# Expert products, gate logits and residual transposes in another order at the end of an attention layer

## What is computed

```python
def _L3_ffn_ref(x, gate_w, gate_b, w1, b1, w2, b2):
    scores = jnp.einsum('bsd,de->bse', x, gate_w) + gate_b
    probs = jax.nn.softmax(scores, axis=-1)
    topk_vals, topk_idx = jax.lax.top_k(probs, TOP_K)
    mask = jnp.sum(jax.nn.one_hot(topk_idx, NUM_EXPERTS, dtype=probs.dtype), axis=-2)
    masked = probs * mask
    masked = masked / (jnp.sum(masked, axis=-1, keepdims=True) + 1e-09)
    h = jax.nn.gelu(jnp.einsum('bsd,edh->ebsh', x, w1) + b1[:, None, None, :], approximate=False)
    y = jnp.einsum('ebsh,ehd->ebsd', h, w2) + b2[:, None, None, :]
    out = jnp.einsum('bse,ebsd->bsd', masked, y)
    return out
...
    t = t + _L3_attn_ref(_ln_t(t), L3_attn_qkv_w, L3_attn_qkv_b, L3_attn_out_w, L3_attn_out_b)
    t = t + _L3_ffn_ref(_ln_t(t), L3_ffn_gate_w, L3_ffn_gate_b, L3_ffn_w1, L3_ffn_b1, L3_ffn_w2, L3_ffn_b2)
```

## Time and profile before

| | us |
|---|---|
| median of three runs | 804.9 (804.72 to 805.72) |
| the profiled execution | 806.04 |
| its span, first to last instruction | 803.8 |
| TensorE busy in it | 743.9 (93%) |
| VectorE, ScalarE, POOL busy | 578.1, 571.6, 253.1 |
| mean granted clock of TensorE | 0.973 |

### The profile page before, as it was taken

The page is one execution under the profiler, slowest core; times in us unless marked ns, Lnnn a source line. Parts: engine busy times, 40 slices in busy tenths (PEclk is TensorE's granted clock), DMA queues, the critical chain, the costliest instruction groups (busy, mean ns, idle before and its releaser), DMA issues.

```text
span 803.8 us, 16948 instructions
## 1 busy us (share of the span) xinstructions
PE 743.9 (93%) x5265; PEld 583.6 (73%) x5265; DVE 578.1 (72%) x1415; ACT 571.6 (71%) x1425; POOL 253.1 (31%) x485
## 2 busy tenths in 40 slices
PE   1896999999999888999998986999999999999997
PEld 1874788788788776777776585677777786777775
DVE  6238677676777567788886798688888735877775
ACT  3323777977777557888886866688888748788785
POOL 1902155565554332121222000131212100544434
PEclk9999899999999999999999998899999959999999
DMA  6000000110110132333230002133333102223220
GB/s 218 1 1 0 1 7 17 20 16 18 20 17 16 26 90 74 90 90 104 80 103 17 0 1 80 51 99 88 102 94 89 29 1 82 50 59 76 63 50 20
DMA packets 60073, 41.36 MB, mean 51 GB/s; under 512 B 33904, under 2 KB 52464, under 8 KB 59888
## 3 DMA queue, kind: packets, MB, share of 16 engines
q1 hardware_dynamic: 60016, 40.63, 19.9%
HBM read 12.24 MB, written 3.21 MB: 19 GB/s over the span
## 4 chain that ended last, share of the span: by engine, by line
PE 77%; DVE 11%; ACT 4%; issue 3%; DMA 2%; SPq 2%; POOL 1%; POOLq 0%; DVEq 0%; ACTq 0%
PE ps L1236 11%; PE ps L990 10%; PE ps L1403 9%; PE ps L1418 8%; PE ps L1091 6%; PE ps L995 5%; PE ps L1075 3%; PE ps L1019 3%; PE ps L1033 3%; PE ps L998 2%; PE ps L1020 2%; SPq L309 2%; DMA qk<-hl 2%; PE ps L940 2%; DVE amax L1861 2%
## 5 line engine op out<-in xcount | busy, mean ns | idle before, releaser
L625 ACT ACTIVATE ee<-ps,nmax 128x128 f32<-128x128 f32 (+1 forms) x576 | 205.2, 445 | 11.5 <-DVE nmax L1592 6.4
L1236 PE MATMUL ps<-w,ee 128*128 128x128 f32 x960 | 134.8, 274 | 2.0 <-ACT big L612 1.9
L1236 PEld LDWEIGHTS ps<-w,ee 128*128 128x128 f32 x960 | 112.8, 143 | 13.6 <-ACT ee L625 2.8
L612 ACT ACTIVATE big<-ps 128x512 f32<-128x512 f32 (+1 forms) x192 | 96.6, 555 | 24.7 <-PE ps L1236 23.0
L1595 DVE TENSOR_REDUCE nmax<-ps 128x2 f32<-128x256 f32 x192 | 97.5, 550 | 13.5 <-PE ps L998 8.9
L1716 DVE TENSOR_TENSOR hhl<-ee,hhl 128x512 fp32r<-128x512 f32 x96 | 79.1, 829 | 33.1 <-ACT hhl L859 31.6
L990 PE MATMUL ps<-kh,big 128*128 128x256 f32 x384 | 94.7, 391 | 1.5 <-POOL big L385 1.2
L1592 DVE TENSOR_REDUCE nmax<-ps 128x4 f32<-128x1024 f32 x48 | 58.7, 1224 | 45.3 <-PE ps L990 45.1
L1403 PE MATMUL ps<-qk,w1hl 128*128 128x512 f32 x288 | 85.4, 405 | 0.0
L1418 PE MATMUL ps<-hhl,w2hl 128*96 128x512 f32 x288 | 82.4, 396 | 2.2 <-DVE big L1946 1.9
L529 POOL TENSOR_TENSOR xc<-big,xc 96x512 f32<-96x512 f32 x32 | 52.1, 1628 | 100.0 <-DVE big L1946 99.4
(11 more groups left out here) (260 smaller groups left out, 1333.2 us busy)
## 6 DMA issues: line engine op xcount, KB each, us to landing
qk<-hl SPq DMA_DIRECT2D x256, 96.0 KB, 3.1
big<-moe_gate SPq DMA_DIRECT2D x8, 768.0 KB, 6.9
w<-w_in SPq DMA_DIRECT2D x1, 1735.0 KB, 12.5
xc<-x_in SPq DMA_DIRECT2D x4, 384.0 KB, 5.6
l_mix<-on SPq DMA_DIRECT2D x32, 48.0 KB, 2.1
tok<-l_mix SPq DMA_DIRECT2D x16, 96.0 KB, 2.0
out<-xc SPq DMA_DIRECT2D x8, 192.0 KB, 2.1
w<-w_in SPq DMA_DIRECT2D x1, 998.0 KB, 8.8
```

The source lines that it names most:

```text
L612: nc.scalar.activation(et[:, h, 0:w], ps[:, 4 + hh, 0:w], ACT.Copy).then_inc(own(l, f"et{hh}"), 1)
L625: last = nc.scalar.activation(ee[:, ke, hh, qc, 0:w], src, ACT.Exp, bias=nmax[:, kp, hh, qc:qc + 1])
L1236: last = nc.tensor.transpose(ps[:, 4 + hh, b * P:(b + 1) * P], ee[:, u, hh, qc, tc * P:(tc + 1) * P], ident)
```

## The change

- TensorE's end of layer 3 follows a table, END_PE, in which three of the H stand between the other steps, and four of the R between the G; the O, C and P of image 15, B of images 14 and 15 and all G are in the table too. `hidden` is defined earlier for that. Four waits that stood in front of single steps stand in front of the table.
- The residual groups go in the order 0 to 7 with other banks; R4 stands before H3, R5 to R7 behind H3 to H5.
- ScalarE makes its split copies before its copy of the attention's result, and its residual copies of groups 0 and 1 after the copy by channel, groups 2 and 3 after the last `deviation`, 4 to 7 behind the first four Gelu pairs. VectorE makes its two `split_low` before it divides image 15.
- The first four gated sums stand in steps 12 to 15 instead of 14 to 17 (all later ones where they stood); the later `split_low` in the fifth step of a block instead of the third; T one pair later, VectorE's copy of it one low part later.
- SyncE waits for the first load of the gates before it issues the second.

```diff
-RES_ORDER = [0, 7, 1, 2, 3, 4, 5, 6]
-RES_BANK = [1, 1, 2, 3, 2, 1, 2, 3]
+RES_ORDER = [0, 1, 2, 3, 4, 5, 6, 7]
+RES_BANK = [1, 2, 3, 1, 2, 3, 2, 3]
+END_PE = ["H0", "O15", "G0", "C15", "H1", "B14", "R0", "P15", "G1", "R1", "H2", "G2", "R2", "G3", "R3", "G4", "B15", "G5", "G6", "G7"]
...
-            return max(NJ * k + 6, 14 + k)
+            return max(NJ * k + 6, 12 + k)
...
             load_gates(0)
+            sp.wait_ge(sg("moe_gates0"), 16)
             load_gates(1)
...
-                if l > 1:
-                    outputs_to_sbuf(l, B - 1)
-                    deviation(l, B - 2, 0)
-                if l == 3:
-                    residual_channels(0)
-                if l > 1:
-                    outputs_by_channel(l, B - 1)
                 if l == 3:
                     for par in range(2):
                         act.wait_ge(*upto(3, f"stacked{par}", STK * B // 2))
                     split_high(0)
                     split_high(1)
+                if l > 1:
+                    outputs_to_sbuf(l, B - 1)
+                    deviation(l, B - 2, 0)
+                    outputs_by_channel(l, B - 1)
+                if l == 3:
+                    residual_channels(0)
+                    residual_channels(1)
                     deviation(l, B - 1, 1)
-                    residual_channels(7)
+                    for g in range(2, 4):
+                        residual_channels(g)
...
-            residual_channels(1)
             for n in range(NS * NB):
...
-                if n < 5:
-                    residual_channels(n + 2)
+                if n < 4:
+                    residual_channels(n + 4)
...
-                    if l == 3:
-                        pe.wait_ge(*upto(l, "max", 3 * B))
-                        pe.wait_ge(*upto(l, "exp", 6 * B))
-                        gate_logits(0)
-                    outputs(l, B - 1)
+                    if l == 2:
+                        outputs(l, B - 1)
...
                 if l == 3:
-                    for g in range(2, 6):
-                        gate_logits(g)
-                    residual_rows(7)
-                    image_back(l, B - 1, 1)
-                    gate_logits(6)
-                    gate_logits(7)
+                    pe.wait_ge(*upto(l, "max", 3 * B))
+                    pe.wait_ge(*upto(l, "exp", 6 * B))
+                    pe.wait_ge(*upto(l, "v_sb", B))
+                    pe.wait_ge(sg("f3_wlo"), 1)
+                    for step in END_PE:
+                        what, n = step[0], int(step[1:])
+                        if what == "H":
+                            hidden(n)
+                        elif what == "G":
+                            gate_logits(n)
+                        elif what == "R":
+                            residual_rows(n)
...
             LAG = 3
-            pe.wait_ge(sg("f3_wlo"), 1)
             pe.wait_ge(sg("f3_w2lo"), 1)
-            for n in range(LAG):
-                hidden(n)
-                residual_rows(n + 1)
+            residual_rows(4)
             for n in range(LAG, NS * NB):
                 hidden(n)
+                if n < 6:
+                    residual_rows(n + 2)
                 expert_out(n - LAG)
-                if n < 6:
-                    residual_rows(n + 1)
-                if n == 6:
+                if n == 7:
                     pe.wait_ge(sg("f3_gate"), 1)
-                    pe.wait_ge(sg("xres"), res_done(3))
+                    pe.wait_ge(sg("xres"), 8)
                     nc.tensor.transpose(ps[:, 3, 0:P], gate[:, 0, :, :].rearrange("p t e -> p (t e)"), ident).then_inc(sg("moe_gate_ps"), 1)
-                if n == 9:
+                if n == 11:
                     pe.wait_ge(sg("moe_gate_t"), 1)
...
+                if l == 3:
+                    for t in range(2):
+                        split_low(t)
                 if l > 1:
                     normalise_outputs(l, B - 1)
...
-                    for t in range(2):
-                        split_low(t)
                     image_channels(l, B - 1)
...
-                if n == 4:
+                if n == 5:
                     dve.wait_ge(sg("moe_gate_ps"), 1)
                     V.tensor_copy(gate_t, ps[:, 3, 0:P]).then_inc(sg("moe_gate_t"), 1)
-                if n % NS == 2 and 1 <= n // NS < NB - 1:
+                if n % NS == 4 and 1 <= n // NS < NB - 1:
                     split_low(n // NS + 1)
```

More of the change, by code:

```diff
@@ L1172, in gate_logits, with hidden @@
                 last.then_inc(sg("f3_gl_ps"), 1)
+            def hidden(n):
+                t, s = n // NS, n % NS
+                if s == 0:
+                    pe.wait_ge(sg("moe_x"), t + 1)
+                if n >= 4:
+                    pe.wait_ge(sg("moe_hi"), n - 3)
+                for k, (w, x) in enumerate(((0, 0), (0, 1), (1, 0))):
+                    last = mm(ps[:, 4 + n % 4, :], w1hl[:, w, s * P:(s + 1) * P], xhl[:, t % 2, x, :], start=(k == 0), stop=(k == 2))
+                last.then_inc(sg("moe_h_ps"), 1)
             for l in (1, 2, 3):
@@ L1330, in _ @@
                     first_layer(0, 0)
-                if l == 3:
-                    gate_logits(1)
-                if l > 1:
+                if l == 2:
                     outputs_back(l, B - 1)
-                if l == 3:
-                    residual_rows(0)
-                if l > 1:
                     pe.wait_ge(*upto(l, "v_sb", B))
@@ L1341, in _ @@
                 if l == 3:
-                    for g in range(2, 6):
-                        gate_logits(g)
-                    residual_rows(7)
-                    image_back(l, B - 1, 1)
-                    gate_logits(6)
-                    gate_logits(7)
+                    pe.wait_ge(*upto(l, "max", 3 * B))
[10 more added lines that the diff above has]
+                            residual_rows(n)
+                        elif what == "O":
+                            outputs(l, n)
+                        elif what == "C":
+                            outputs_back(l, n)
+                        elif what == "B":
+                            image_back(l, n, n % 2)
+                        else:
+                            project_outputs(l, n)
                 if l > 1:
@@ L1395, in _ @@
                                 last.then_inc(sg("f2_y2_ps"), 1)
-            def hidden(n):
-                t, s = n // NS, n % NS
-                if s == 0:
-                    pe.wait_ge(sg("moe_x"), t + 1)
-                if n >= 4:
-                    pe.wait_ge(sg("moe_hi"), n - 3)
-                for k, (w, x) in enumerate(((0, 0), (0, 1), (1, 0))):
-                    last = mm(ps[:, 4 + n % 4, :], w1hl[:, w, s * P:(s + 1) * P], xhl[:, t % 2, x, :], start=(k == 0), stop=(k == 2))
-                last.then_inc(sg("moe_h_ps"), 1)
             def expert_out(n):
@@ L1414, in expert_out @@
                     pe.wait_ge(sg("f3_gl"), 1)
-                if j == 0 and t == 0 and 1 <= e <= 2:
-                    pe.wait_ge(sg("xres"), 6 + e)
+                if j == 0 and t == 0 and e > 0:
+                    pe.wait_ge(sg("xres"), max(res_done(g) for g in range(8) if RES_BANK[g] == e))
                 for k, (w, h) in enumerate(((0, 0), (1, 0), (0, 1))):
```

## The result

Five executions of the changed kernel have a median of 798.29 us (797.83 to 800.84), five of the kernel before beside them 804.72 (802.17 to 805.72). The ratio is 0.9938, with a 95% interval of 0.9922 to 0.9955: 5.0 us faster (3.6 to 6.3).

A forecast was written before the change was run, and what follows sets the result against it. TensorE, hardly ever without work from 640.50 us, was taken as the bound. -2.9 - 0.35 + 2.3 - 1.93 = -2.9 gave 803.1 from the profiled 806.04; the median 804.9 - 1.93 gave 802.97; forecast 803.0, range 801.0 to 805.2.

The forecast's parts named there:

- The wait before E(12), -1.93: TensorE's idle before E(12), waiting for the first gated sum, goes with the earlier gated sums: 1.93 us less, or 1.6.
- The order of the end: Layer 3's end on TensorE: early H delay the clock's fall to 651.43, last G ends at 655.27, E0 starts 2.9 earlier.
- gate chain: From the last G's end to E0, top-2 gate and low_part(0): 4.94 us plus 0.13, no longer covered by H and R.
- new wait: TensorE idle before E0, with only R4, H3 and R5 as cover: 2.2 us, or 3.6 at full clock.
- The clock after E0, +2.3: TensorE reaches E0 at half clock, and 3.2 to 5.7 us of products at half rate lose 1.6 to 2.9; 2.3 taken.
- first rival: The clock stays up through layer 3's end: 798.0 us on the median; falling but back by E0, near 800; chance 0.14.
- My two cases for its return: Full clock returns 3.2 us after gapless work from 478.0, or 5.7 us after dense products began at 656.37.
- the clock's terms: The sum's -2.9, -0.35 and +2.3 at layer 3's end, -0.95 together, left out when forecasting from the median.
- the sum: Whole kernel, from the profiled execution: -2.9 - 0.35 + 2.3 - 1.93 = -2.9 us, so 806.04 becomes 803.1.
- The second rival: The clock falls as early as before, H not holding it; last G ends at 660.7, total 807.5, slower; chance 0.10.
- the third one: Middle rival: the clock falls near 650, returns late, gate load takes 7.7; 805.4 us, no change; chance 0.26.
- The rule on transposes: Transposes don't count as clock activity like products, so only the H among the logits hold it; lowers the first rival's chance.

The follow-up runs named there:

- third profile of the same kernel: The changed kernel run a third time, nothing edited: median 798.89 us, ratio 0.9933 to the kernel before; its profiled execution took 801.92 us.
- steps alone: The kernel before with only the first four gated sums moved to steps 12 to 15: 801.63 us, ratio 0.9973.
- All but the steps: The changed kernel with the first four gated sums back in steps 14 to 17: 802.33 us, ratio 0.9974 to the kernel before.
- late H: The changed kernel with H0, H1 and H2 behind the last G again, run twice: 798.66 us (ratio 0.9934) and 799.24 us (0.9937).
- H and R both late: The changed kernel with H0 to H2 and R1 to R3 behind the last G, ScalarE's residual copies moved along: 799.18 us, ratio 0.9953.
- second profile of that kernel: The changed kernel run again, nothing edited: median 799.49 us, ratio 0.9936 to the kernel before; its profiled execution took 799.93 us.
- H3 three times: The changed kernel with H3 computed three times into the same bank before E0, R5 ahead of it: 797.58 us, ratio 0.9918.
- H2 late: The changed kernel with H2 alone moved behind the last G, into the wait before E0: 796.07 us, ratio 0.9903.

## Why the prediction was wrong

**The wait before E(12), -1.93: right.** Alone it brought 2.2, undone it cost 2.8. The gates came in time, a little sooner than I had worked out: the load landed near 676.4 and the first gated sum ran 8.71 after T (676.43 against 667.72), where I had the load landing 9.05 after it. VectorE waited for it, as I had said, though only 0.24 us.

**The order of the end: the mechanism right, the sizes small.** H0 came without a wait and takes 0.80 (O starts at 640.58), as priced. The clock fell 10.3 us after A, forecast 10.9. The last G ended 14.13 after A, forecast 14.77: G costs 0.81 between R (645.91 to 646.72), not 0.95. The gate chain took 5.02 from there to E0 (653.91 to 658.93), forecast 4.94 + 0.13. The new wait is 1.83, forecast 2.2; E0 came 19.15 after A, forecast 19.84. Against 22.73 before that is 3.6 earlier instead of 2.9.

**The clock after E0, +2.3: too much.** I had it low from the fall until some 4.6 us behind E0. In the changed kernel it was back before E0, at the end of R5, and then fell once more for 3.4 us, which costs 1.7. That is the first rival's last sentence (it falls and is back by E0: near 800), to which I had given part of 0.14; the profiled execution took 800.84. In the third profile of the same kernel it didn't come back, as forecast. My two cases for its return, 3.2 and 5.7 us, I had both called dense products. In the second, three H and two R stood in turn from 656.37 to 662.1, so it was no such case; and that it returns with only one H among transposes was in no row I had.

**The step that failed: the clock's terms, mis-sized in the sum and then put at nothing on the median.** On the profiled execution the sum gave -2.9; measured was -5.2. Of the 2.3 between them, 0.7 is A, which the change doesn't touch and which was 638.8 to 640.5 in all profiles, 0.7 lies from A to E0 (G and the wait), and 0.9 behind E0 (the return, above all). On the median I then struck out the clock's terms, -0.95, as the part by which the profiled execution was the longer one, and wrote 803.0 twice. That agreement was of my own making: one was the time of a profiled execution and the other a median. The profiled execution is longer than the median of its kernel in 13 of the 14 profiles here, by 0.2 to 3.9 us, before and after alike, so that the difference of two profiles is no excess to be struck out; and the long low stretch stood in the profile of steps alone too (17.1 us, the same order on TensorE). All but the steps, the part that I had struck out, brought 2.1 on the median (0.6 to 3.6), and by the recorded clock of 49 and 17 executions the changed order has 5.8 us less of low clock in the mean, which is 2.9 us. Had I kept the terms, the forecast would have been 802.0; the rest is their size.

**The range.** Its lower end, 801.0, left out nearly all of the first rival. One program's profiles here differ by 3.4 us of low clock in the changed order and by 13.7 with late H, that is 1.7 and 6.9 us of time before anything else varies. A range that rests on the moment of a clock's fall has to be as wide as that on both sides; mine reached 2.2 up and 2.0 down.

**The rivals.** That the median, 798.3, lies at the first rival's 798.0 is chance: its sum has no low clock at the end, and the three profiles have 10.2 to 13.6 us of it. The second rival needed a fall before 648.0 and the third one near 650 with a late return, that is before 7.5 and near 9.5 us after A. The changed kernel's falls came 10.2, 10.3 and 11.0 after A, around the forecast 10.9, so the second didn't come; nor did the third, and in the two with the earlier falls the clock was back before E0, not late.

**Readings that were wrong without weight in the sum.** I wrote that four R had stood between the last G and E0 before; it was three. I wrote that four R had stood in the 3 us before 645.04; it was one R, of four transposes.

**The rule on transposes.** I had used the Trainium skill (TensorE: Matmul & The Clock Gate, Part 4: PE-mode transpose) to lower the first rival's chance: transposes don't count as activity for the clock as products do. The runs leave it open. With late H the clock stood at 1.00 until 651.1, with only logits, transposes and one small projection (P) since 640.38, in one execution, and fell at 642.1 in the other. I should not have moved a chance by it.

**What stays open.** What sets the moment of the fall in one execution; and which of the moved H and R keep the low clock short, since late H alone have nearly the changed kernel's low clock (37.6 us against 36.7 in the mean) and H and R both late have more (40.6), by few executions each.

## What to carry to other kernels

Take the low-clock stretch of a profile as a cost of half its busy length, and count what a change does to it on the median as on the profile; don't call it chance because an execution was long. Before giving a range that hangs on a clock's fall, profile the kernel more than once: the same program here had 3.4 and 17.1 us of it. When independent products move ahead of a chain to hold the clock, keep as many behind it as its length needs: two H ahead and one behind had a lower median than three ahead or three behind, by 2.8 and 3.2 us, in six executions of each, with intervals that still overlap.

## What the runs showed of the hardware

The clock fell at 650.1 among the logits and, the logits over at 653.91, returned to 2.4 GHz at 656.9, while TensorE ran four transposes, three products and four transposes. It stayed there through 1.83 us of idle, and was lost again 1.5 us after work had begun (660.4). The same pattern stood in the second profile of that kernel (back at 656.0, lost at 659.4), while after the 1.93 us wait of the kernel before it was not lost at all. The waits are about equally long; ahead of it stood some 19 us at full clock, nearly all of them products of 512 columns, in the one case (662.1 to 681.6), and logits, transposes and a single H in the other. With products in the wait (H3 three times, H2 late) the second fall was gone, in one profile each; the recorded clock of their six executions each agrees (31.8 and 32.6 us in all against 36.7).
